# The last node stage of a graph network layer: how the two row normalisations take their sums, how far inputs and routed rows are buffered, and where the router's scale is applied

## The reference

```python
x1 = x + gnn(xn) + mix(xn)                 # gnn ends: relu(layernorm(gat(h)) * g + b + h)
h  = layernorm(layernorm(x1)) * gamma + beta
logits = h @ Wr + br                       # 8 experts, the two greatest are kept
y  = sum over the two experts of weight * expert(h)
out = x1 + y
```

## Time and profile before

| | us |
|---|---|
| median of three runs | 7522.47 |
| lowest and highest of them | 7515.94, 7524.8 |
| the profiled execution | 7531.31 |
| its span, from the first to the last instruction | 7529.6 |

### The profile page before, as it was taken

The page is one execution under the profiler, slowest core; times in us unless marked ns, Lnnn a source line. Parts: engine busy times, 40 slices in busy tenths (PEclk is TensorE's granted clock), DMA queues, the critical chain, the costliest instruction groups (busy, mean ns, idle before and its releaser), DMA issues. The chain is left out here.

```text
span 7529.6 us, 113108 instructions
## 1 busy us (share of the span) xinstructions
PE 5390.2 (72%) x23828; PEld 3495.0 (46%) x23829; DVE 5498.7 (73%) x16160; ACT 2138.7 (28%) x5415; POOL 5176.0 (69%) x5471
## 2 busy tenths in 40 slices
PE   5677777766775677777766666587777876673399
PEld 3344444444443345444544444355555544342398
DVE  6677777777777677777777778677787777778643
ACT  2112121211113233333321113234343421113466
POOL 1777777777774777777777773777777777772444
PEclk8777787877778777777777777678888877776599
DMA  6445455544443444444444444444444444444444
GB/s 211 138 141 145 141 146 141 144 135 140 136 134 116 117 121 123 121 123 122 122 114 111 111 110 139 115 123 128 126 128 125 127 118 111 111 111 139 146 70 64
DMA packets 531615, 949.93 MB, mean 126 GB/s; under 512 B 117850, under 2 KB 366049, under 8 KB 531030
## 3 DMA queue, kind: packets, MB, share of 16 engines
q0 software_dynamic: 259808, 691.84, 34.5%
q1 hardware_dynamic: 254610, 235.89, 10.2%
q10 hardware_dynamic: 16612, 15.96, 0.6%
HBM read 796.92 MB, written 151.73 MB: 126 GB/s over the span
## 5 line engine op out<-in xcount | busy, mean ns | idle before, releaser
L1250 POOL DMA_INDIRECT edges_G<-rows,edges_index x4980 | 4749.4, 954 | 1554.4 <-issue 1481.0
L1450 PE MATMUL edges_ps_o<-edges_G,edges_OH 128*128 128x264 f32 x9960 | 3507.1, 490 | 307.1 <-DVE edges_G L1726 173.9
L1450 PEld LDWEIGHTS edges_ps_o<-edges_G,edges_OH 128*128 128x128 f32 x9960 | 2119.1, 234 | 1127.4 <-issue 634.9
L1744 DVE TENSOR_TENSOR acc<-acc,edges_ps_o 128x264 f32 x2490 | 1048.8, 421 | 821.7 <-PE edges_ps_o L1450 547.6
L1726 DVE TENSOR_TENSOR edges_G<-edges_G,edges_ps_c 128x1024 f32<-128x1024 f32 x1245 | 1500.3, 1205 | 1.8 <-ACT edges_G L1270 1.3
L1294 ACT ACTIVATE edges_OHT<-edges_ps_far 128x512 bf16<-128x512 f32 x1245 | 742.5, 596 | 1331.2 <-PE edges_ps_far L1410 1330.8
L1418 PE MATMUL edges_ps_s<-ident,edges_alpha 128*128 128x128 f32 x249 | 114.4, 459 | 1266.5 <-DVE edges_alpha L1620 1266.5
L1718 DVE TENSOR_TENSOR edges_OH<-edges_ps_c,relT 128x512 f32<-128x512 f32 x1245 | 848.6, 682 | 0.1
L1602 DVE COPY edges_node<-terms 128x12 bf16 x2490 | 476.1, 198 | 292.1 <-issue 73.8
L1418 PEld LDWEIGHTS edges_ps_s<-ident,edges_alpha 128*128 128x128 f32 x249 | 44.2, 177 | 1375.3 <-DVE edges_alpha L1620 1375.3
L1410 PE MATMUL edges_ps_far<-edges_rels,pole_rows 5*128 5x512 bf16 x1245 | 608.4, 489 | 41.3 <-DMA WT<-in_L_mix_b 19.8
(11 more groups left out here) (377 smaller groups left out, 6211.3 us busy)
## 6 DMA issues: line engine op xcount, KB each, us to landing
edges_G<-rows,edges_index POOLq DMA_INDIRECT x4980
xslot<-edges_blank SPq DMA_DIRECT2D x80, 650.0 KB
edges_masks<-lanes_of SPq DMA_DIRECT2D x123, 192.0 KB
rows<-node_ext SPq DMA_DIRECT2D x147, 130.0 KB, 2.2
experts_X<-xslot SPq DMA_DIRECT2D x105, 130.0 KB, 2.1
node_rows<-rows SPq DMA_DIRECT2D x98, 130.0 KB
h<-node_Hn SPq DMA_DIRECT2D x98, 128.0 KB, 1.7
W<-in_L_ffn_W SPq DMA_DIRECT2D x16, 512.0 KB
```

The lines of the kernel that those rows point to most:

```text
L1250: g.indirect_dma_start(G[n][:, s, 0:RW], None, dr["rows"], bass.IndirectOffsetOnAxis(index[n][:, s:s + 1], 0)).then_inc(gathered[n], 16)
L1450: mm = pe.matmul(ps_o[BANK_OF[g]][:, 0:GW], OH[:, 2 * g + j, :], G[n][:, 2 * g + j, :], start=(j == 0), stop=(j == 1))
L1744: v.tensor_tensor(a, a, ps_o[BANK_OF[g]][:, 0:GW], ALU.add).then_inc(added, 1)
```

## The change

The row sums are no longer taken by bn_stats. The operation that adds the two parts of a tile in `gather` becomes a scalar_tensor_tensor that also gives the sum of each row (`accum_out`, into `total1`), and the one that makes `Hn` in `finish` gives its sum likewise (`total2`). bn_stats and bn_aggr go. ScalarE computes the mean (an Identity of one column) and the sum of squares of `sum - 256 x` (a Square with `accum_out`) before its square root; the constants are divided out in the square root's scale. For the second norm it does the same from `Hn`. Both write the squares themselves to a tile `square` that nobody reads. `gather` has three steps instead of five, `finish` five instead of seven, and `second` waits one step before its reciprocal instead of three. A tile has four rounds instead of six, and the batch takes one step after the first and third, two after the second and fourth.

`rows`, `prev` and `mix` become rings of eight (`AHEAD`), and SP issues the loads of tiles 4 to 7 behind those of the router's constants. `XH` holds three batches. The waits for the constants move behind the first two tiles' `gather` on VectorE and behind their `std` on ScalarE. The router's scale goes into its weights: before the loop ScalarE makes `Wg = gamma * Wr` and a tile `shift` that holds `beta` in every column, PE multiplies `shift` by `Wr`, and VectorE adds that to `br`. `spread` is then a single copy, and `route` uses `Wg`.

```diff
     BATCHES = NB // BATCH
-    KEEP = 2 * BATCH
+    KEEP = 3 * BATCH
+    AHEAD = 2 * TILE_RING
     LAG = 5
     with Phase(nc, "final") as ph:
-        rows = ph.sb("rows", [P, TILE_RING, RW])
-        prev = ph.sb("prev", [P, TILE_RING, C])
-        mix = ph.sb("mix", [P, TILE_RING, C])
+        rows = ph.sb("rows", [P, AHEAD, RW])
+        prev = ph.sb("prev", [P, AHEAD, C])
+        mix = ph.sb("mix", [P, AHEAD, C])
...
-        loaded = [ph.sem(f"loaded{k}") for k in range(TILE_RING)]
+        loaded = [ph.sem(f"loaded{k}") for k in range(AHEAD)]
         x2_out = [ph.sem(f"x2_out{k}") for k in range(TILE_RING)]
...
             def load(b):
-                slot = b % TILE_RING
+                slot = b % AHEAD
                 for to, of in ((rows, "rows"), (prev, "h"), (mix, "mix")):
...
                 sp.dma_start(beta[:, :], io["ffn_beta"].rearrange("(k p) -> p k", p=P)).then_inc(router_in, 16)
+            for b in range(TILE_RING, AHEAD):
+                load(b)
             for b in range(NB):
...
                 sp.dma_start(out[b * P:b * P + tail(b), :], Hn[0:tail(b), b % TILE_RING, :]).then_inc(x2_out[b % TILE_RING], 16)
-                if b + TILE_RING < NB:
-                    load(b + TILE_RING)
+                if b + AHEAD < NB:
+                    load(b + AHEAD)
                 if b % 4 == 3 and b // 4 < EX:
...
             c0.link(v.tensor_copy(total[:, :, 0], region[:, :]))
-            v.wait_ge(vecs_in, 32)
-            v.wait_ge(router_in, 64)
             def gather(b):
-                slot = b % TILE_RING
-                v.wait_ge(loaded[slot], 16 * 3 * (b // TILE_RING + 1))
+                slot, place = b % TILE_RING, b % AHEAD
+                v.wait_ge(loaded[place], 16 * 3 * (b // AHEAD + 1))
                 o = O[:, slot, :]
...
                 e, z = (es[:, k, b, :].unsqueeze(2).broadcast_to([P, H, D]) for k in range(2))
-                c1.add(v.tensor_tensor(oh, by_head(rows[:, slot, :])[:, :, 0:D], e, ALU.mult))
+                c1.add(v.tensor_tensor(oh, by_head(rows[:, place, :])[:, :, 0:D], e, ALU.mult))
                 yield
...
                 c1.wait()
-                c1.add(v.tensor_tensor(oh, oh, a, ALU.add))
-                yield
-                c1.wait()
-                c1.add(v.bn_stats(stats[:, slot, :], o))
-                yield
-                c1.wait()
-                v.bn_aggr(mv[:, slot, :], stats[:, slot, :]).then_inc(stats_ready, 1)
+                v.scalar_tensor_tensor(out=oh, in0=oh, scalar=1.0, in1=a, op0=ALU.mult, op1=ALU.add,
+                                       accum_out=total1[:, slot, :]).then_inc(stats_ready, 1)
...
                 c2.wait()
-                c2.add(v.scalar_tensor_tensor(out=o, in0=prev[:, slot, :], scalar=0.0, in1=o, op0=ALU.max, op1=ALU.add))
+                c2.add(v.scalar_tensor_tensor(out=o, in0=prev[:, b % AHEAD, :], scalar=0.0, in1=o, op0=ALU.max, op1=ALU.add))
                 yield
...
                     v.wait_ge(xhat_ready, b - TILE_RING + 1)
-                v.scalar_tensor_tensor(out=hn, in0=o, scalar=0.0, in1=mix[:, slot, :], op0=ALU.max, op1=ALU.add).then_inc(x2_ready, 1)
-                yield
-                v.wait_ge(x2_ready, b + 1)
-                c2.add(v.bn_stats(stats2[:, slot, :], hn))
-                yield
-                c2.wait()
-                v.bn_aggr(mv2[:, slot, :], stats2[:, slot, :]).then_inc(stats2_ready, 1)
+                v.scalar_tensor_tensor(out=hn, in0=o, scalar=0.0, in1=mix[:, b % AHEAD, :], op0=ALU.max, op1=ALU.add,
+                                       accum_out=total2[:, slot, :]).then_inc(x2_ready, 1)
...
                 slot = b % TILE_RING
-                for _ in range(3):
-                    yield
+                yield
                 v.wait_ge(sd2_ready, b + 1)
...
                 c3.wait()
-                v.tensor_scalar(shift2[:, slot, :], mv2[:, slot, 0:1], scale2[:, slot, :], -1.0, ALU.mult, ALU.mult
+                v.tensor_scalar(shift2[:, slot, :], total2[:, slot, :], scale2[:, slot, :], -1.0 / C, ALU.mult, ALU.mult
                                 ).then_inc(shift2_ready, 1)
...
                 yield
-                if q >= 2:
+                if q >= KEEP // BATCH:
                     for slot in range(ring, ring + BATCH):
-                        v.wait_ge(scattered[slot], 16 * 2 * (q // 2))
+                        v.wait_ge(scattered[slot], 16 * 2 * (q // (KEEP // BATCH)))
                 meta = XH[:, ring:ring + BATCH, C:XW]
...
                     pass
+            v.wait_ge(vecs_in, 32)
+            v.wait_ge(router_in, 64)
+            v.wait_ge(shared, 1)
+            v.tensor_tensor(br[:, :], br[:, :], psR[:, 0:EX], ALU.add).then_inc(br_ready, 1)
+            v.wait_ge(br_ready, 1)
             for b in range(NB + 1):
...
                 done[0] = b
-                for _ in zip_longest(*turns):
-                    next(batches, None)
+                for turn, _ in enumerate(zip_longest(*turns)):
+                    for _ in range(1 + turn % 2):
+                        next(batches, None)
             done[0] = NB
...
                          ACT.Exp).then_inc(es_ready, 1)
-            a.wait_ge(router_in, 64)
-
             def std(b):
...
                 a.wait_ge(stats_ready, b + 1)
-                a.activation(sd[:, slot, :], mv[:, slot, 1:2], ACT.Sqrt, bias=eps[:, :]).then_inc(sd_ready, 1)
+                a.activation(mv[:, slot, 0:1], total1[:, slot, :], ACT.Identity, scale=1.0 / C).then_inc(squared, 1)
+                a.activation(square[:, :], O[:, slot, :], ACT.Square, bias=total1[:, slot, :], scale=-float(C),
+                             accum_out=mv[:, slot, 1:2]).then_inc(squared, 1)
+                a.wait_ge(squared, 2 * b + 2)
+                a.activation(sd[:, slot, :], mv[:, slot, 1:2], ACT.Sqrt, bias=eps[:, :], scale=1.0 / C ** 3).then_inc(sd_ready, 1)
...
                 slot = b % TILE_RING
-                a.wait_ge(stats2_ready, b + 1)
-                a.activation(sd2[:, slot, :], mv2[:, slot, 1:2], ACT.Sqrt, bias=eps2[:, :], scale=1.0 + LN_EPS).then_inc(sd2_ready, 1)
+                a.wait_ge(x2_ready, b + 1)
+                a.activation(square[:, :], Hn[:, slot, :], ACT.Square, bias=total2[:, slot, :], scale=-float(C),
+                             accum_out=mv2[:, slot, 1:2]).then_inc(squared2, 1)
+                a.wait_ge(squared2, b + 1)
+                a.activation(sd2[:, slot, :], mv2[:, slot, 1:2], ACT.Sqrt, bias=eps2[:, :], scale=(1.0 + LN_EPS) / C ** 3).then_inc(sd2_ready, 1)
...
                     a.wait_ge(logits, b - 1)
-                for k in range(2):
-                    ins = a.activation(xs[:, b % 2, k, :], psA[b % 2][:, k * P:(k + 1) * P], ACT.Identity,
-                                       bias=beta[:, k:k + 1], scale=gamma[:, k:k + 1])
-                ins.then_inc(xs_ready, 1)
+                a.copy(xs[:, b % 2, :, :].rearrange("p k n -> p (k n)"), psA[b % 2][:, 0:C]).then_inc(xs_ready, 1)
...
                 std(b)
+            a.wait_ge(router_in, 64)
+            for k in range(2):
+                a.activation(shift[:, k, :], ident[:, :], ACT.Identity, bias=beta[:, k:k + 1], scale=0.0).then_inc(folded, 1)
+            for k in range(2):
+                a.activation(Wg[:, k, :], Wr[:, k, :], ACT.Copy, scale=gamma[:, k:k + 1]).then_inc(folded, 1)
             for b in range(NB + 2):
...
             pe.wait_ge(router_in, 64)
+            pe.wait_ge(folded, 4)
+            for k in range(2):
+                mm = pe.matmul(psR[:, 0:EX], shift[:, k, :], Wr[:, k, :], start=(k == 0), stop=(k == 1))
+            mm.then_inc(shared, 1)
...
                 for k in range(2):
-                    mm = pe.matmul(psL[q % 2][:, b % BATCH * EX:(b % BATCH + 1) * EX], xs[:, b % 2, k, :], Wr[:, k, :],
+                    mm = pe.matmul(psL[q % 2][:, b % BATCH * EX:(b % BATCH + 1) * EX], xs[:, b % 2, k, :], Wg[:, k, :],
                                    start=(k == 0), stop=(k == 1))
...
```

More of the change, by code:

```diff
@@ L2002, in final_phase @@
     BATCHES = NB // BATCH
-    KEEP = 2 * BATCH
+    KEEP = 3 * BATCH
+    AHEAD = 2 * TILE_RING
     LAG = 5
     with Phase(nc, "final") as ph:
-        rows = ph.sb("rows", [P, TILE_RING, RW])
-        prev = ph.sb("prev", [P, TILE_RING, C])
-        mix = ph.sb("mix", [P, TILE_RING, C])
+        rows = ph.sb("rows", [P, AHEAD, RW])
+        prev = ph.sb("prev", [P, AHEAD, C])
+        mix = ph.sb("mix", [P, AHEAD, C])
         O = ph.sb("O", [P, TILE_RING, C])
         Hn = ph.sb("Hn", [P, TILE_RING, C])
-        stats = ph.sb("stats", [P, TILE_RING, 6])
+        total1 = ph.sb("total1", [P, TILE_RING, 1])
+        total2 = ph.sb("total2", [P, TILE_RING, 1])
+        square = ph.sb("square", [P, C])
         mv = ph.sb("mv", [P, TILE_RING, 2])
@@ L2014, in final_phase @@
         rstd = ph.sb("rstd", [P, TILE_RING, 1])
-        stats2 = ph.sb("stats2", [P, TILE_RING, 6])
         mv2 = ph.sb("mv2", [P, TILE_RING, 2])
@@ L2031, in final_phase @@
```

(10 more changed lines are left out.)

## The result

The changed kernel takes **7481.07 us** (7478.19 to 7485.08) against 7522.47: a ratio of 0.9947, with an interval of 0.9933 to 0.9962, so 41 us less (29 to 50). The forecast was 7495. Its profiled execution took 7485.1 us with a span of 7483.3; the edges' phases ahead of the stage, which nobody touched, ended 9.7 us earlier in it than in the one of before, so the stage has to be read by its own length.

A forecast was written before the change was run, and what follows sets the result against it. VectorE, issuing without a gap, was taken to bound the stage's loop. Nine plain periods 29.1, five sevens 139.0 and four last 15.5 gave 183.6 against 210.8, -27: 7495 from 7522.5; range 7480 to 7524, the forecast's own 7480 to 7507.

The forecast's parts named there:

- What bounds it, and one for one to the end: Final stage: VectorE issues without a gap, GpSimd's 28 scatters end it; loop savings move the end equally unless scatters pile up.
- The ring of VectorE and ScalarE: Dependent steps through both engines, row sums to variances to reciprocal, set a plain tile at 3.23 us, 0.40 less.
- VectorE alone: VectorE's own work in a plain tile after the change, apart from waiting for ScalarE: 2.93 us, from 3.63.
- The wait behind Exp: Once a batch ScalarE loads tables for Exp and back to Sqrt; VectorE then waits 1.93 us for the second variance.
- Logits: Once a batch VectorE waits about 1.5 us for the router's logits; that tile takes 4.69 us to its row sum.
- the routing tile: A tile that also carries routing steps of a batch: 3.59 us, with 0.1 for steps that depend on each other.
- both reads at nothing: Lower case: reading the row sums costs nothing on either engine, VectorE sets the pace, loop 172 us, time 7483.
- Buffers: Eight tiles of inputs remove 8.5 us of `mix` waits; three batches of `XH` remove ScalarE's 7.0 us scatter wait.
- The start "within 1 us": Ahead of the loop, the dropped `beta` wait of 4.3 us and the new folded-bias wait balance within 1 us; nothing counted.
- Half rate: Rival: a row sum halves the adding operation's rate, 0.27 us more each; loop 205, time 7516 to 7522; chance 0.17.
- Loads late all the same: Rival: DMA loads don't keep up and the wait for `mix` stays at 8.5 us; time 7504; chance 0.06.
- Square outside Sqrt's table: Rival: Square needs another ScalarE table, four loads of 1.28 us a tile, +190 us, about 7710; chance 0.07.

The follow-up runs named there:

- f1: Changed kernel with the second reciprocal and shift two steps later and each batch's routing begun one tile later: 7466.89 us, loop 160.3.
- e5: Changed kernel with one more small square root on ScalarE, between the second Square and its square root: 7483.7 us (single execution), loop 179.7.
- e7: Changed kernel with the second reciprocal and shift back two steps later in VectorE's tile: 7474.1 us (single execution), loop 168.7.
- e4: Changed kernel without the two row sums, the adding operations having no accumulator: 7479.5 us (single execution), loop 173.7.
- e6: Changed kernel with a Square in place of the Exp that weighs each token's two experts: 7476.0 us (single execution), loop 169.7.
- e1: Kernel before with only the change's buffers, a ring of eight input tiles and three batches of rows: 7503.35 us, loop 196.1.
- e3: Changed kernel with the old buffers, four tiles of inputs and two batches of rows kept: 7513.09 us, loop 208.6.
- f3: Changed kernel with the router scale out of the weights, ScalarE spreading each tile with two operations: 7479.9 us (single execution), loop 177.5.
- f2: Against f1, two routing steps in every place of a tile that had one and two by turns: 7486.4 us, loop 179.9.

## Why the forecast was right, and where its sizes were off

- **What bounds it, and one for one to the end: right.** The loop lost 36.2, the stage 37.0; 28 scatters in a row end it. They start 5.3 us behind the last x2. The condition, that earlier scatters don't pile up, holds in the change with 4.0 us to spare (the idle time in the row above) and no longer in f1.
- **The ring of VectorE and ScalarE: right as a mechanism, mis-sized.** 3.23 was reckoned for a plain tile, 2.89 measured. By the timeline: Square starts 0.14 behind the row sum's end, its read ends 0.10 after the Square (6860.84 and 6860.74) where I had put 0.20, twice; VectorE's sum is ready with its operation, where I had put 0.10; each Square takes 0.02 less. That is 0.20 + 0.10 + 0.04 = 0.34. The step that failed is the one that priced a read, on either engine, as an operation standing behind its source: 0.20 on ScalarE, where 0.10 is added, and 0.10 on VectorE, where nothing is. "Plain tiles of 2.9 would mean that ScalarE's reads hide": half of each does. The wait of about 0.3 a tile for the second square root, which was to be seen on VectorE, is 0.02. e5 shows that the ring is still there, with no room.
- **VectorE alone: right in sum, by luck.** 2.93 reckoned, 2.92 in e7, by terms that were not right: the reads, 0.16, are all but free (e4), and in their place L2232 now waits for L2228 with nothing between (0.52 from start to start in e7, where a statistics operation filled that time before).
- **The wait behind Exp: right place, 1.93 for 0.88.** ScalarE was 0.39 earlier than reckoned (the reads again) and VectorE 0.67 later, partly for its 0.37 wait for the ranks, which the forecast didn't have. e6 and e7 both take it away.
- **Logits: 1.5 reckoned, 1.25 measured; the routing tile 3.59 reckoned, 3.3 to 3.6 measured** where no wait stands in it. The terms given for the logits' tile add up to 4.76 and not to the 4.69 used; 4.56 was measured.
- So the loop: nine plain tiles 26.0 for 29.1, five sevens 133.8 for 139.0, the last four 14.8 for 15.5: 174.6 for 183.6. These sizes are 9 of the 14 us between 7495 and 7481; the start gives 1, the end takes 0.5, and the rest, some 4, is no larger than the spread of the runs. The end "both reads at nothing", 7483, came nearest, though ScalarE's read does add 0.10 and the loop is 174.6 and not 172.
- **Buffers: right** (e1: 14.7 for 15.5). What the forecast didn't say is that they carry the rest: without them the faster tile is worth 2.2 us (e3).
- **The start "within 1 us": about right, by terms that cancel** (first x2 16.75 behind the stage's start, 17.85 before), out of -3.7 for the moved wait (14.1 in f3) and 2.6 for the fold.
- **The rivals.** Half rate: refuted by 406 against 407 ns (e4). The rule of the Trainium skill ("Vector Engine (DVE) Microarchitecture Reference", section 7), half throughput for this operation with two sources that aren't bf16, isn't borne out by that. Loads late all the same: refuted for a ring of eight, true for four (33.8 us). Square outside Sqrt's table: refuted, and more than that:

```profile
6890.07 0.21 ACT L2444 ACTIVATE final_ex<-final_gap 128x7 f32<-128x7 f32 x1
6890.18 0.19 ACT L2411 ACTIVATE final_mv<-final_total 128x1 f32<-128x1 f32 x1
6890.27 0.49 ACT L2412 ACTIVATE final_square<-final_O,final_total 128x256 f32<-128x256 f32 x1
6890.67 0.19 ACT L2412 ACTIVATION_READ_ACCUMULATOR final_square<-final_O,final_total 128x1 f32 x1
6890.88 1.28 ACT L2415 ACT_TABLE_LOAD   x1
```

Square runs right behind Exp, and the load comes only for Sqrt: it ran under either table. The Trainium skill ("ScalarE: Activation LUTs", "Table sets: the hidden batching unit") says that cheap functions are in every set; Square isn't among the four it names for that, and here it behaves like one of them in the two sets that this kernel loads there.

Open: how far the phases ahead of the stage vary by themselves, and why. The logits put ahead of the next tile's turn on TensorE, which the last rows under f3 suggest, weren't tried, nor were the ranks of f2 moved forward on TensorE.

## What to carry to other kernels

An improvement can be worth little without another: here a faster tile without the deeper buffers mostly waited for its loads and brought 2.2 us, and 21.5 with them. The lead of a ring of buffers is what lies between a slot's release and its next use, one tile here and not four. Where work is moved to another engine, write out the cycle through both, since a step inside it lengthens every turn once there is no slack (0.18 for an operation of 0.29 in e5); then look for a step that can leave the cycle (`second`, 5.9 us) before shortening one. And before a step is moved ahead on one engine, look where the engine that answers it has that answer in its queue (f2).

## What was not expected of the hardware

The accumulator is read by an instruction of its own, 82 ns on VectorE and 187 on ScalarE. VectorE's read starts together with the next operation, and the loop is only 0.9 us shorter without all 98 of them; ScalarE's begins 0.09 before its Square ends and adds 0.10 to the chain. An adding operation of two fp32 tensors with a row sum runs as fast as one without, 406 and 407 ns.
